# Second expert layer of a two-block decoder: rows scattered by expert group by group, loaded back by SyncE, in place of a gather list

## The reference, cut to what matters

```python
xf = x.reshape(-1, 128)                                      # 2048 tokens
gate_logits = selu(xf @ gate_wi + gate_bi) @ gate_wo + gate_bo
topv, topi = top_k(gate_logits, 2)                           # the first 8 of 128 columns are experts:
topv = topv / sum(topv)                                      # a choice of 8 or more counts for nothing
onehot = (topi[..., None] == arange(8))
w = einsum('nk,nke->ne', topv, onehot)
h = selu(einsum('nh,ehf->enf', xf, exp_wi) + exp_bi)         # 8 experts, 128 -> 512
out_e = einsum('enf,efh->enh', h, exp_wo) + exp_bo           # 512 -> 128
out = einsum('enh,ne->nh', out_e, w)
x = x + out
```

## Time and profile before

| | us |
|---|---|
| median of 3 runs (lowest, highest) | 945.34 (942.3, 950.31) |
| profiled execution | 953.9 |
| its span, first to last instruction | 952.2 |
| gate of the second expert layer, to the last choice | about 743 to 783 |
| lists | 783 to 802 |
| expert loop, first gather to last scatter | 802.4 to 938.2 |
| results back, added and stored | 939.5 to 952 |

### The profile page before, as it was taken

One profiled execution on the slowest core, in us unless ns is written; L12 is line 12 of the kernel. 1 busy time (PEld: TensorE's weight loads), 2 busy tenths in 40 slices (PEclk: granted clock), 3 DMA queues, 4 the chain that ended last, 5 costly groups with the idle time before them and its releaser, 6 DMA issues.

```text
span 952.2 us, 16029 instructions
## 1 busy us (share of the span) xinstructions
PE 787.6 (83%) x5413; PEld 592.3 (62%) x5413; DVE 688.2 (72%) x1414; ACT 485.6 (51%) x946; POOL 543.0 (57%) x550
## 2 busy tenths in 40 slices
PE   9987777777797768999989699999989989687772
PEld 7462222222367757888867577867666778676672
DVE  7479999999978432444799767769999796345554
ACT  4857666676553113662562223256665920555662
POOL 6669999999944631553299434564443002465652
PEclk9979999999999589999999799999999999789997
DMA  8991000000033212213000000000000302744544
GB/s 221 186 198 51 1 0 0 1 0 1 1 112 106 68 50 64 71 41 114 1 1 1 1 1 1 1 1 2 12 14 25 113 22 56 98 119 110 129 123 149
DMA packets 65849, 53.86 MB, mean 57 GB/s; under 512 B 7115, under 2 KB 56921, under 8 KB 65770
## 3 DMA queue, kind: packets, MB, share of 16 engines
q1 hardware_dynamic: 61002, 43.04, 18.7%
q0 software_dynamic: 4768, 9.81, 5.1%
HBM read 29.26 MB, written 21.47 MB: 53 GB/s over the span
## 4 chain that ended last, share of the span: by engine, by line
PE 33%; DVE 17%; POOL 8%; issue 7%; ACT 5%; another core or an unknown queue 4%; DMA 1%; ACTq 0%; DVEq 0%; POOLq 0%
PE ps L2480 4%; PE ps L2164 3%; PE ps L2489 3%; PE ps L1878 2%; PE ps L2290 2%; PE ps L1863 2%; PE ps L2173 2%; DVE small L1654 2%; PE ps L2345 2%; DVE G L1657 1%; POOL R L616 1%; PE ps L1885 1%; PE ps L1958 1%; DVE R L1615 1%
## 5 line engine op out<-in xcount | busy, mean ns | idle before, releaser
L519 POOL TENSOR_TENSOR R<-G,R 128x1024 f32<-128x1024 f32 x43 | 100.7, 2357 | 8.6 <-ACT R L777 4.5
L1292 DVE TENSOR_TENSOR_SCAN R<-ps,R 128x1024 f32<-128x1024 f32 x43 | 97.7, 2280 | 10.2 <-POOL R L528 5.5
L1863 PE MATMUL ps<-ident 128*128 128x128 f32 x714 | 93.2, 292 | 3.0 <-POOL ident L487 1.8
L836 ACT ACTIVATE ps<-G,negAb,negA 128x508 f32<-128x508 f32 x128 | 95.0, 779 | 0.5 <-DVE R L1292 0.5
L1863 PEld LDWEIGHTS ps<-ident 128*128 128x128 f32 x714 | 90.1, 208 | 5.7 <-POOL ident L487 1.8
L1937 PE MATMUL ps<-bc,sel 96*128 96x512 bf16 x128 | 46.1, 387 | 47.4 <-ACT LN L784 23.0
L1958 PE MATMUL ps<-R,ident 128*128 128x512 f32 x172 | 82.0, 599 | 0.0
L1937 PEld LDWEIGHTS ps<-bc,sel 96*128 96x128 bf16 x128 | 12.5, 97 | 98.8 <-ACT LN L784 36.0
L701 POOL DMA_INDIRECT G<-xn_rows,token x39 | 39.0, 1000 | 57.8 <-DVE per_tile L1817 45.3
L777 ACT COPY R<-ps 128x512 f32<-128x512 f32 x64 | 37.5, 586 | 66.2 <-PE ps L1937 66.2
L1827 DVE TENSOR_TENSOR G<-ps,biasT 128x512 f32<-128x512 f32 x39 | 26.6, 685 | 56.3 <-PE ps L2480 30.6
(11 more groups left out here) (422 smaller groups left out, 2136.2 us busy)
## 6 DMA issues: line engine op xcount, KB each, us to landing
R<-in_exp_wi_dram SPq DMA_DIRECT2D x39, 256.0 KB
rows_by_expert<-blank SPq DMA_DIRECT2D x8, 1040.0 KB, 17.8
G<-in_w_dram SPq DMA_DIRECT2D x24, 128.0 KB, 2.5
y_rows<-blank SPq DMA_DIRECT2D x1, 2048.0 KB, 14.7
G<-LN SPq DMA_DIRECT2D x8, 256.0 KB
G<-first_y_rows SPq DMA_DIRECT2D x4, 512.0 KB, 6.4
xn_rows<-LN SPq DMA_DIRECT2D x8, 256.0 KB
G<-in_exp_wo_dram SPq DMA_DIRECT2D x8, 256.0 KB, 4.5
```

The lines of the kernel that those rows point to most:

```text
L519: gp.tensor_tensor(halves(dBu[i % 3]), duT[:, :, gcols(i // NS)], Bsb[:, i % 4:i % 4 + 1, :].broadcast_to([P, HI, GT]), ALU.mult).then_inc ...
L836: sc.activation(bank(2 * j + m)[:, 0, :].rearrange("p (b t) -> p b t", b=GB)[:, :, 1:T], dT[:, m, gcols(g)].rearrange("p (b t) -> p b t", ...
L1292: v.tensor_tensor_scan(hst[i % 3], bank(2 * j, 2).rearrange("p h n -> p (h n)"), dBu[i % 3], 0.0, ALU.mult, ALU.add).then_inc(S["scanned"], 1)
L1863: mm(bank(o)[:, 0, 0:P], ident[:], ident[:], start=True, stop=True)
```

## The change

- The second expert layer gets a table of its own in HBM, `second_rows_by_expert`, laid out as the first layer's with 4224 rows ahead of it (`NO_EXPERT`), to which pairs without an expert go, each to a row of its own. SP fills it with blank rows at the start, behind the first table: nine more transfers, 8.8 MB.
- SP copies each group's normalized tokens within SBUF to `rows1[g]` twice (`stage`) in place of the store to HBM; POOL writes each row's destination (iota), DVE its weight, and POOL scatters 8 blocks per group as soon as `index1` says that the group's places are known: 32 indirect transfers in all.
- The lists fall away: DVE's 32 one-hots and the two wide products, PE's 32 list matmuls, the counts over all groups. In their place each group has three or four small matmuls (`rows_at`) and four short DVE operations (`find_rows`), and the plan of tiles is that of the first layer.
- The 39 gathers on POOL become 39 loads of 128 rows on SP, six issued ahead and then each between two loads of up weights, all behind register loads.
- ACT's copy of the down weights falls away (39 copies of 128 x 512): PE reads the resident table at the expert of the tile, with a register load on PE.
- `logits(0)` stands ahead of `gate_up(2)`; the transposes of gate weights and the products with the folded bias leave the loop and stand ahead of it, followed by `unread(7, 60)` where `unread(7, 24)` stood.
- DVE makes `goes_to` tile by tile, one more 128 x 1 operation per tile.

SP's queue around the up weights (`R<-in_exp_wi_dram`), before: once the tile's expert is known (`wc_done` is here the plan), a register load and its transfer, again and again.

The core of the diff:

```diff
+            for dram in (row_dram, row1_dram[NO_EXPERT:]):
+                for first in range(0, ROWS, N):
...
-            store_xn(NG - 1)
-            wait(sp, "eid_rdy", 1)
-            for i in range(NT):
+            sp.wait_ge(S["hw_res"], B)
+            stage(NG - 1)
+            wait(sp, "plan2", 1)
+            def load_up(i):
                 e = sp.value_load(tile_e[0:1, i:i + 1], min_val=0, max_val=E - 1)
                 if i >= 4:
                     sp.wait_ge(S["up1_mm"], i - 3)
-                sp.dma_start(wi[:, i % 4, :], a["exp_wi"][bass.ds(e, 1), :, :].rearrange("e p n -> (e p) n")).then_inc(S[f"wi_in{i % 4}"], 16)
+                sp.dma_start(wi_now[:, i % 4, :], a["exp_wi"][bass.ds(e, 1), :, :].rearrange("e p n -> (e p) n")).then_inc(S[f"wi_in{i % 4}"], 16)
+            def load_rows(i):
+                first = sp.value_load(token[0:1, i:i + 1], min_val=0, max_val=NO_EXPERT + E * N + 6 * P)
+                if i >= 4:
+                    wait(sp, f"xm{i % 4}", 16 * (i // 4))
+                sp.dma_start(row1_at(i), row1_dram[bass.ds(first, P), :]).then_inc(S[f"xm{i % 4}"], 16)
+            for i in range(4):
+                load_up(i)
+            sp.wait_ge(S["rows1_sent"], 16 * 2 * B)
+            for i in range(6):
+                load_rows(i)
+            for i in range(4, NT + 2):
+                if i < NT:
+                    load_up(i)
+                if i + 2 < NT:
+                    load_rows(i + 2)
...
-            wait(pool, "xn_out", 32 * NG)
-            wait(pool, "lst_rdy", 1)
-            for i in range(AHEAD):
-                gather(i)
...
+            for g in range(NG):
+                pool.wait_ge(S["index1"], g + 1)
+                wait(pool, "rows1_in", 32 * (g + 1))
+                for b in range(GB):
+                    for k in range(2):
+                        j = k * B + g * GB + b
+                        gp.indirect_dma_start(row1_dram[:, :], bass.IndirectOffsetOnAxis(ap=per_pair_i[:, j:j + 1], axis=0), rows1[g][:, b, k, :], None)\
+                            .then_inc(S["rows1_sent"], 16)
...
+            def find_rows(g):
+                dve.wait_ge(S["placed1"], g + 1)
...
+                v.tensor_tensor(by_choice(per_pair_i[:]), by_choice(per_pair[:]), by_choice(pair_id[:]), ALU.max).then_inc(S["index1"], 1)
...
-                    sc.copy(wo_now[:, i % 4, :], wo[:, bass.ds(e * H1, H1)]).then_inc(S["wo_cp"], 1)
...
+            logits(0)
             gate_up(2)
-            logits(0)
...
+            pe.wait_ge(S["eb_res"], NG)
+            unread(7, 60)
             wait(pe, "bt_ev", 2)
+            wait(pe, "plan2", 1)
...
-                    wait(pe, "wo_cp", i + 1)
+                    e = pe.value_load(tile_e[0:1, i:i + 1], min_val=0, max_val=E - 1)
```

More of the change, by code:

```diff
@@ L707, in scatter @@
                     .then_inc(S["y_sent"], 16)
-            wait(pool, "xn_out", 32 * NG)
-            wait(pool, "lst_rdy", 1)
-            for i in range(AHEAD):
-                gather(i)
-            wait(pool, "y_zero", 16)
-            wait(pool, "lst_rdy", 2)
-            for i in range(NT):
-                if i + AHEAD < NT:
-                    gather(i + AHEAD)
-                scatter(i)
         @block.scalar
@@ L1723, in choose @@
[L1723 to L1729 removed]
+                chosen = by_batch(router[:, 3, bs].rearrange("p b e -> p (b e)"))
@@ new lines, in choose @@
+                step(v.tensor_scalar(chosen, rank, 1.5, None, ALU.is_lt))
+                v.tensor_tensor_scan(counted[:], again[:], router[:, 3, bs].rearrange("p b e -> p (b e)"), 0.0, ALU.mult, ALU.add)\
+                    .then_inc(S["chosen1"], 1)
+                dve.wait_ge(S["chosen1"], g + 1)
+                if g:
+                    v.tensor_tensor(taken[:, g], taken[:, g - 1], by_batch(counted[:])[:, GB - 1], ALU.add)
+                else:
+                    v.tensor_copy(taken[:, 0], by_batch(counted[:])[:, GB - 1])
@@ L1774, in _ @@
[L1774 to L1780 removed]
+            find_rows(2)
+            choose(3)
+            weigh(3)
@@ L2452, in _ @@
             mm(bank(0)[0:E, 0, 0:D], ident[0:E, 0:E], w["exp_bo"][:], start=False, stop=True).then_inc(S["ebo_mm"], 1)
-            unread(7, 8)
-            wait(pe, "a1_rdy", 1)
-            for j in range(2 * B):
-                wait(pe, "oh_rdy", j + 1)
-                ins = mm(bank(1)[:, 0, 0:2 * NT], of_pair[:, j], of_tile_vw[:, j].rearrange("p i a -> p (i a)"),
-                         start=j == 0, stop=j == 2 * B - 1)
-            ins.then_inc(S["lst_mm"], 1)
+            rows_at(NG - 1)
@@ L2465, in _ @@
             wait(pe, "ebo_ev", 1)
+            pe.wait_ge(S["gl_cw"], NG)
+            for g in range(NG + 1):
+                if g < NG:
+                    if g:
+                        pe.wait_ge(S["wt_ev"], g)
+                    for b in range(GB):
+                        ins = nc.tensor.transpose(bank(6)[0:E, 0, b * T:(b + 1) * T], cw1[:, g * GB + b, :], ident[:])
+                    ins.then_inc(S["wt_mm"], 1)
+                if g:
+                    pe.wait_ge(S["wt_ev"], g)
+                    if g >= 2:
+                        pe.wait_ge(S["eb_res"], g - 1)
+                    for b in range(GB):
+                        ins = mm(bank(7)[:, 0, b * D:(b + 1) * D], cwT[:, (g - 1) * GB + b, :], bo_fold[:], start=True, stop=True)
+                    ins.then_inc(S["eb_mm"], 1)
```

308 lines of the change are left out of this document (138 added, 170 removed).

## The result

Twenty runs of each kernel side by side: 941.74 us median (937.62 to 946.67) against 948.4 (941.89 to 952.33); the ratio is 0.9938, with a 95% interval of [0.9918, 0.9958]. That is 6 to 7 us or 0.6% less, where 1.4% was forecast. The sign was right, the size less than half.

What follows compares the result with a forecast made beforehand. POOL's gathers were taken to delay PE's results, 3.0 us a tile; afterwards SP's issues bound the loop. Start 826 plus 96.8 gave 922.8 against 936.4, 13.6 us less: 932 us, range 908 to 955.

Steps and rivals of the forecast that it cites:

- SP's two issues: Tile loop: two transfers per tile, each behind a register load, make SP the bound at 2.55 us per tile.
- F: Start of the tile loop: time when DVE reads the first up product, 818.2 before, forecast 826.
- F + 96.8: End of the tile loop: last tile scaled 96.8 us after the first up product is read, where it was 118.2.
- the 0.31 us: Tile loop: extra SP time per POOL scatter beside its issues; 35 of them sum to 10.9 us.
- 826 for lateness: Loop start: 820.5 without delay, 829.5 with one burst delay; 826 taken because six results handed over can each be late.
- The third term: Ahead of the loop: 64 records of transposes and folded bias, 7.5 us, plus 0.5 for DVE between.
- the 13.6 us: Whole kernel: forecast saving, last tile at 922.8 against 936.4.
- SP's side of the start: Before the loop: first scatter at 765, SP loads rows from 814.4, making the loop start about 820.
- Rival D: Before the loop: scatter burst serializes the groups, first up product at 858, 18.4 us more, 964; chance 0.13.
- Rival B: Start and loop: no burst effect on PE, SP undisturbed, last tile at 905.9, 30.5 us less, 915; chance 0.20.
- C: Tile loop: something that stays, not the gathers, holds PE; pace 3.0 a tile, 7.8 us more, 953; chance 0.12.
- The items at nothing: ACT's dropped copies, PE's register load, DVE's `goes_to`, bias products leaving the loop and second blank fill, all priced at zero.

Runs made afterwards that it cites:

- f3: Kernel before the change with only the first ten gathers, later tiles computed on what stands there: 916.74 us, one run, beside 949.57.
- e4: Changed kernel with SP loading up weights for the first four tiles only, so one issue per tile: 932.15 us, one run, beside 948.22 before the change.
- e8: Changed kernel with a 128 x 512 memset behind each of POOL's 32 row scatters: 931.82 us, one run, beside 946.6 before the change.
- e3: Changed kernel without POOL's 32 scatters of rows and SP's wait for them: 930.09 us, one run, beside 948.22 before the change.
- e1: Changed kernel without the 60 unread matmuls ahead of the tiles: 926.43 us, ratio 0.9786 to the kernel before the change.
- f4: Kernel before the change with all 39 gathers issued ahead of the first scatter: 953.53 us, one run, beside 949.57.
- e6: Changed kernel with gate weights and folded bias among the tiles again and no unread matmuls: 918.8 us, ratio 0.9711 to the kernel before the change.
- e12: e6 with a 128 x 128 memset behind each scatter of the first three groups: 897.19 us, ratio 1.0011 to the kernel before the change.
- e9: Kernel before the change with only the first ten gathers, on the chip of 897.29 us: 881.96 us, one run.

## Why the prediction was right and where it was wrong

**Right: what bounds the tiles, before and after.** The gathers held PE's results (f3, 33 us, with the waits beside it), and SP's two issues are the new bound (e4). The last tile was to end at F + 96.8; it ended at F + 85.9. The mis-sized term is the 0.31 us that each scatter was to cost SP: 68 issues took 1.14 each, 77 us in place of 76.2 + 10.9. That price was read beside scatters issued in a row; at one scatter in 2 us nothing of it is left, as e8 shows too.

**Wrong: where F lies.** The step summed PE's side to 820.5 and took 826 for lateness; it was 842.7. By its own terms, measured in the trace after:

| term | forecast | measured |
|---|---|---|
| last places and total ready | 792.9 | 797.6 |
| plan, bias product | 4.8 | 5.5 |
| gate weights and folded bias | 8.0 | 21.3 (803.2 to 824.4) |
| 60 unread matmuls | 14.0 | 16.5 |
| first transpose and product | 0.8 | 1.8 |

The third term failed: 13.3 of the 22.2 us. 8.20 of them are the wait up to 814.92, POOL's holding as in the earlier trace rows, which the forecast had put at 5.5 for the whole stretch. In e8, where nothing was held, the same stretch still took 14.4 us (798.00 to 812.40), 6.4 more than forecast, so about half of the miss is there without any holding. That half is the clock of 0.50, at which eight records of products last 2.0 us and not 0.9, and the hand-over between PE and DVE, which the forecast gave 0.5 us for eight. The clock fell while PE waited so much, and the unread matmuls too began at the lower level. Without POOL's burst (e3) the tiles still begin only at 827.7, since bias products, low clock and unread matmuls remain.

**That the sign came out right is luck.** A start 16.7 us later than the 826 of the forecast was offset by a loop 10.9 us shorter than its 96.8, and 5.8 of the 13.6 us were lost. With the start as it was and the loop as forecast, the last tile would have ended at 842.7 + 96.8 = 939.5, 3.1 later than before the change.

**The larger error of the same step is one of attention, not of size:** the 14 us of unread matmuls were in the sum and nobody waited for what they brought. They count alone for 15 us (e1), two and a half times what the change gained.

**SP's side of the start was right:** first scatter 764.2 (forecast 765), rows asked for at 815.28 (814.4), POOL with gaps of 3.3 and 4.2 us only between groups. Rival D, the groups taking turns with the burst, was seen in small: F stayed 6 us short of the 849 from which it would have been slower. Rival B had the loop right (76.2 + 9.7 = 85.9) and the start wrong. C is refuted by f3 on the slower kind of chip: scatters, loads of up weights, copies and bias products are all there, and the tiles last 80.5 us. f4 adds that scatters hold PE too once they follow each other without a pause. The items at nothing held: e4's pace leaves no room for PE's register load, and the first scatter of the first layer stands at 298.5 in both kernels, so the second blank fill cost nothing.

The Trainium skill says that DMA never contends with a compute engine ("SBUF — State Buffer", "Who interferes with whom"), in a section on SBUF's ports. Taken for a rule on who waits for whom, it speaks for C. On the chips of 947 to 950 it is no guide to what PE does beside POOL's indirect transfers: without POOL's transfers, or with a pause between them, the same PE program is 13 to 15 us earlier (e3, e8).

**Open:** by which way POOL's transfers hold PE and SP. PE's results come late and PE itself stands still in pieces of about a microsecond, and SP's issues stretch from 1.1 to about 4 us; no row names what they wait for. Open too is why one chip of the four on which experiments ran doesn't show it.

## What to carry to other kernels

Work that moves out of a loop into its prologue is priced by the prologue's own conditions: low clock, hand-overs that nothing covers, a neighbour's burst; here 21 us for what hid in the loop (83.0 us of tiles in e6, against 81.6 in e1). Warm-up matmuls are to be taken out and timed whenever what stands around them changes. Before a chain of indirect transfers is issued in a row, look at what other engines hand over meanwhile; half a microsecond of other work on POOL between two of them freed PE and SP in e8 and moved the last one by 7 us. Whether it pays where the last scatter sets the start, as in e6, is not shown: e12 ran only on the chip where nothing was held. And if a result rests on such an effect, compare on more than one chip.

## What of the hardware was not expected

Beside indirect transfers of POOL every 1.26 us SP's issues came (12.48 - 0.34) / 3 = 4.0 us apart instead of 1.1, and beside transfers every 1.79 us they came as fast as alone (3.72 us for four, 3.68 without any). One chip ran the unchanged kernel in 897.29 us, 5% below the 946.6 to 949.57 of the others; in e9, whose first layer is that of the kernel before, the first layer's scatters came every 41.1 / 31 = 1.33 us instead of 1.47, and the tiles after them ended 23 us earlier (the last of their results was scattered at 417.4, not 440.8). The tiles' own matmuls brought the clock back as well as unread ones had: the granted clock from 824 to 841 is 0.80 in e1 and 0.81 in the changed kernel.
